# A mixture-of-experts stage on one core: results scattered by tile, later register loads, and three unused matmuls

## What is computed

```python
logits = x @ gate_w + gate_b
probs = jax.nn.softmax(logits, axis=-1)
topv, topi = jax.lax.top_k(probs, K)                 # K = 2 of E = 8 experts
topv = topv / jnp.sum(topv, axis=-1, keepdims=True)
comb = jnp.sum(topv[..., None] * jax.nn.one_hot(topi, E), axis=2)
h = gelu(jnp.einsum('bnd,edf->bnef', x, w1) + b1)    # 192 -> 768
y = jnp.einsum('bnef,efd->bned', h, w2) + b2         # 768 -> 192
ffn_out = jnp.einsum('bne,bned->bnd', comb, y)
out = layernorm(x + ffn_out + bk_scale * (feats @ out_w + out_b))
```

## Time and profile before

| | us |
|---|---|
| median of 3 runs | 229.34 |
| lowest and highest | 228.66 and 230.13 |
| profiled execution, device time | 229.1 |
| its span, first to last instruction | 227.2 |
| PE busy / DVE / POOL / ACT in it | 161.9 / 102.2 / 75.2 / 47.6 |
| mean granted TensorE clock | 0.852 of full |

### The profile page before, as it was taken

How to read it: one execution, slowest core, us unless ns; L and a number is a source line. 1 busy time by engine, 2 the same in 40 slices (tenths; PEclk the granted TensorE clock), 3 DMA queues, 4 the chain that set the end, 5 groups by cost and what they waited for, 6 DMA issues and landing times.

```text
span 227.2 us, 2861 instructions
## 1 busy us (share of the span) xinstructions
PE 161.9 (71%) x928; PEld 133.6 (59%) x928; DVE 102.2 (45%) x302; ACT 47.6 (21%) x89; POOL 75.2 (33%) x196
## 2 busy tenths in 40 slices
PE   0999998888888827610212999999999999993000
PEld 0677754455555415610102899999999999992000
DVE  1129994998899494472103122222332222203445
ACT  0353344343111203210000111232111231110000
POOL 1799300000000121027668877882000000004761
PEclk9999999999999965555555699999999999997555
DMA  6990499999990000003265001000000000011222
GB/s 217 331 408 13 116 265 261 250 261 257 272 341 22 0 1 0 0 0 117 82 197 186 0 5 33 18 19 20 17 31 24 17 20 17 17 38 44 77 56 80
DMA packets 14932, 23.46 MB, mean 103 GB/s; under 512 B 1599, under 2 KB 11396, under 8 KB 14790
## 3 DMA queue, kind: packets, MB, share of 16 engines
q1 hardware_dynamic: 12800, 19.80, 29.9%
q0 software_dynamic: 928, 2.09, 3.0%
q10 hardware_dynamic: 1190, 1.38, 1.9%
HBM read 17.96 MB, written 5.31 MB: 102 GB/s over the span
## 4 chain that ended last, share of the span: by engine, by line
PE 65%; DVE 11%; issue 9%; POOL 5%; DVEq 4%; DMA 3%; ACT 1%; POOLq 0%
PE ps L965 20%; PE ps L975 14%; PE ps L814 8%; PE ps L822 7%; PE ps L823 5%; PE ps L868 4%; POOL diag_s L398 4%; DVEq L746 4%; PE ps L802 3%; DMA w1t_s<-in_w1t 2%; DVE conv L570 1%; DVE stats L616 1%; DVE conv L582 1%; POOL rstd L378 1%; DVE zt L647 1%
## 5 line engine op out<-in xcount | busy, mean ns | idle before, releaser
L965 PE MATMUL ps<-conv 128*128 128x128 f32 x384 | 48.2, 285 | 6.9 <-DVE conv L751 6.5
L965 PEld LDWEIGHTS ps<-conv 128*128 128x128 f32 x384 | 47.3, 201 | 7.6 <-issue 6.8
L570 DVE SCALAR_TENSOR_TENSOR conv<-conv,vecs 128x240 f32<-128x240 f32 (+1 forms) x94 | 35.9, 444 | 7.3 <-ACT conv L447 6.8
L975 PE MATMUL ps<-w_s,conv 128*128 x192 | 33.7, 326 | 0.0
L760 DVE COPY arena<-ps 128x192 f32<-128x192 f32 x16 | 5.7, 358 | 57.5 <-PE ps L975 57.5
L975 PEld LDWEIGHTS ps<-w_s,conv 128*128 128x128 f32 x192 | 30.9, 190 | 0.0
L398 POOL DMA_INDIRECT diag_s<-slot_results,slots x10 | 9.6, 961 | 54.9 <-DMA slot_results<-arena 52.1
L378 POOL TENSOR_TENSOR rstd<-var,neghalf 128x2 f32<-128x2 f32 (+1 forms) x6 | 4.8, 807 | 62.9 <-DVE var L622 62.9
L507 ACT COPY conv<-ps 128x256 f32<-128x256 f32 x16 | 6.0, 373 | 82.8 <-PE ps L956 82.8
L751 DVE COPY conv<-w_s 128x1536 f32 x16 | 15.2, 957 | 14.5 <-issue 9.5
L822 PE MATMUL ps<-conv,pw_s 128*128 128x288 f32 (+1 forms) x48 | 17.4, 445 | 5.5 <-DVE conv L582 3.8
(11 more groups left out here) (152 smaller groups left out, 185.8 us busy)
## 6 DMA issues: line engine op xcount, KB each, us to landing
w_s<-in_w SPq DMA_DIRECT2D x8, 576.0 KB, 18.1
w_s<-in_w SPq DMA_DIRECT2D x8, 384.0 KB
slot_rows<-zero SPq DMA_DIRECT2D x1, 2048.0 KB, 22.2
arena<-in_x SPq DMA_DIRECT2D x4, 432.0 KB, 9.6
w_s<-in_w SPq DMA_DIRECT2D x8, 192.0 KB
slot_results<-arena SPq DMA_DIRECT2D x16, 96.0 KB, 1.6
pw_s<-in_pw SPq DMA_DIRECT2D x1, 1152.0 KB, 11.5
arena<-slot_rows SPq DMA_DIRECT2D x1, 1024.0 KB, 7.6
```

What stands on the lines that cost most here:

```text
L570: ins = nc.vector.scalar_tensor_tensor(out=o, in0=a, scalar=w, in1=o, op0=ALU.mult, op1=ALU.add)
L965: last = mm(p1_ps[i % 2][:, c * P:(c + 1) * P], w1_cur[:, i % 2, k * F + c * P:k * F + (c + 1) * P], xs[:, i % 2, k * P:(k + 1) * P], star ...
L975: last = mm(y_ps[i % 2], hT[:, i % 2, k * P:(k + 1) * P], w2_flat[:, bass.ds(expert[i] * (FK * D) + k * D, D)], start=(k == 0), stop=(k == ...
```

## The change

There are four parts.

1. The destination goes with the row. `ht` becomes one half of `sent`, ScalarE makes the second half, and column 193 carries the row of `yd` where the pair's result belongs: 1 + 2 x token for the first choice, 2 + 2 x token for the second. Slots that hold no pair have a zero there and get a spare row behind all others. When all five pieces of `xg` are there, DVE turns the column into `home`, one destination for each slot.
2. The results are scattered tile by tile. POOL stores the results of tile i with an indirect DMA as soon as they are ready, where SP stored them in slot order. `yd` then lies in token order, and the ten gathers of POOL become plain loads of 192 KB on SP (tiles 0, 2, 4) and ScalarE (tiles 1, 3, and one broadcast row for the class tokens). POOL begins the scatters after its spectral part.
3. The register loads move. PE's 16 come behind the transposes of `combp`; DVE's go into the loop, one ahead of each weight copy.
4. PE multiplies `id_s` by three 384-column slices of `w2_s` into a bank of `p1_ps[1]`, which nobody reads, before it waits for the rows of tile 0.

```diff
--- before.py
+++ after.py
@@ -57,7 +57,8 @@
 
 
 R_TRI, R_ONE, R_THR, R_IOTA, R_VALID = 0, 2 * P, 3 * P, 3 * P + E * E * NT, 3 * P + E * E * NT + S * (E - 1)
-NROUTE = R_VALID + NT * E
+R_HOME, R_SPARE = R_VALID + NT * E, R_VALID + NT * E + 2 * NT
+NROUTE = R_SPARE + S
 
 
 def tower(nc, x, vec, rows, had, w1t, plw, pw, projw, cls, ident, layout, route, w1, b1, w2, b2, outw, xd, yd, out):
@@ -98,7 +99,8 @@
         diag = diag_s[:].rearrange("p (f t m k) -> p f t m k", f=3, t=2, m=3)
 
         zt = sb("zt", [P, NT, D])
-        ht = sb("ht", [P, NT, XW])
+        sent = sb("sent", [P, 2, NT, XW])
+        ht = sent[:, 0]
         stats = sb("stats", [P, NT, 6])
         mv = sb("mv", [P, NT, 2])
         var = sb("var", [P, NT])
@@ -247,6 +253,12 @@
             hi = min(P * (groups[g][-1] + 1), end)
             return slice(lo, hi), slice(0, hi - lo)
 
+        def load_y(queue, t):
+            w = min(P, K1 - t * P)
+            row = 1 + 2 * t * P
+            queue.dma_start(yg[0:w, t, :, :],
+                            yd[row:row + 2 * w, :].rearrange("(p c) d -> p c d", c=2)).then_inc(d_yg[t], 16)
+
         block = ctx.enter_context(nc.Block())
 
 
@@ -274,9 +286,9 @@
             sp.wait_ge(d_sent, 16 * 2 * NT)
             for k, (a, b) in enumerate(pieces):
                 sp.dma_start(xg[:, a:b, :], xd[a * P:b * P, :].rearrange("(i p) c -> p i c", p=P)).then_inc(d_xg[k], 16)
-            for i in range(S):
-                sp.wait_ge(y_rdy, i + 1)
-                sp.dma_start(yd[i * P:(i + 1) * P, :], xg[:, i, 0:D]).then_inc(d_yd, 16)
+            sp.wait_ge(d_yd, 16 * S)
+            for t in (0, 2, NT - 1):
+                load_y(nc.sync, t)
             for t in (0, 2, NT - 1):
                 sp.wait_ge(fin_rdy, t + 1)
                 w = min(P, TOK - P * t)
@@ -361,7 +373,7 @@
                         nc.gpsimd.tensor_scalar(diag[:, f, t, m, :], id_s[:], vecs[:, tap:tap + 1], None,
                                                 ALU.mult).then_inc(diag_rdy, 1)
 
-            nc.gpsimd.memset(ht[:, :, D:XW], 0.0).then_inc(padded, 1)
+            nc.gpsimd.memset(sent[:, :, :, D:XW], 0.0).then_inc(padded, 1)
             nc.gpsimd.memset(combp[:], 0.0).then_inc(padded, 1)
             pool.wait_ge(diag_rdy, 18)
             pool.wait_ge(padded, 2)
@@ -369,8 +381,11 @@
             nc.gpsimd.memset(w1_s[HI, :, 1, :], 0.0).then_inc(w1_zero, 1)
             pool.wait_ge(padded, 3)
             pool.wait_ge(w1_zero, 1)
-            nc.gpsimd.memset(ht[:, :, D:D + 1], 1.0).then_inc(padded, 1)
+            nc.gpsimd.memset(sent[:, :, :, D:D + 1], 1.0).then_inc(padded, 1)
             nc.gpsimd.memset(combp[:, :, SPEC - 1:SPEC], 1.0).then_inc(padded, 1)
+            pool.wait_ge(d_route, 16)
+            nc.gpsimd.tensor_copy(sent[:, :, :, D + 1],
+                                  route_s[:, R_HOME:R_HOME + 2 * NT].rearrange("p (c t) -> p c t", c=2)).then_inc(padded, 1)
 
             def inverse_root(k, grp):
                 ts = (slice(0, 2), slice(2, NT))[grp]
@@ -380,24 +395,25 @@
             for k, grp in enumerate((0, 0, 1, 1)):
                 inverse_root(k, grp)
             pool.wait_ge(d_clear, 16)
-            pool.wait_ge(padded, 5)
+            pool.wait_ge(padded, 6)
             pool.wait_ge(ht_rdy, NT)
+            pool.wait_ge(copied, 1)
             pool.wait_ge(slots_rdy, 2)
             for t in range(NT):
                 w = min(P, K1 - t * P)
                 for c in range(2):
                     nc.gpsimd.indirect_dma_start(
                         out=xd, out_offset=bass.IndirectOffsetOnAxis(ap=slots[0:w, c, t:t + 1], axis=0),
-                        in_=ht[0:w, t, :], in_offset=None).then_inc(d_sent, 16)
+                        in_=sent[0:w, c, t, :], in_offset=None).then_inc(d_sent, 16)
             pool.wait_ge(d_sent, 16 * 2 * NT)
             spectral(pool)
+            pool.wait_ge(home_rdy, 1)
+            for i in range(S):
+                pool.wait_ge(y_rdy, i + 1)
+                nc.gpsimd.indirect_dma_start(
+                    out=yd, out_offset=bass.IndirectOffsetOnAxis(ap=home[:, i:i + 1], axis=0),
+                    in_=xg[:, i, 0:D], in_offset=None).then_inc(d_yd, 16)
             pool.wait_ge(d_yd, 16 * S)
-            for t in range(NT):
-                w = min(P, TOK - t * P)
-                for c in range(2):
-                    nc.gpsimd.indirect_dma_start(
-                        out=yg[0:w, t, c, :], out_offset=None, in_=yd,
-                        in_offset=bass.IndirectOffsetOnAxis(ap=slots[0:w, c, t:t + 1], axis=0)).then_inc(d_yg[t], 16)
             inverse_root(4, 0)
             inverse_root(5, 1)
 
@@ -494,6 +510,9 @@
                 act.wait_ge(xt_mm, 2 * g + 2)
                 nc.scalar.copy(xf[LO, 1, c], xb_ps[g][LO, cp]).then_inc(xf_rdy, 1)
 
+            act.wait_ge(ht_rdy, NT)
+            nc.scalar.copy(sent[:, 1, :, 0:D], ht[:, :, 0:D]).then_inc(copied, 1)
+
             act.wait_ge(lg_max, 1)
             nc.scalar.activation(comb[:], lg[:], ACT.Exp).then_inc(lg_exp, 1)
             act.wait_ge(zeroed, 1)
@@ -512,6 +531,13 @@
                     nc.scalar.activation(hT[:, (i - 1) % 2, :], p1_ps[(i - 1) % 2],
                                          ACT.Gelu_apprx_tanh).then_inc(hT_rdy, 1)
 
+            act.wait_ge(d_yd, 16 * S)
+            row = 1 + 2 * (K1 - 1)
+            act.dma_start(yg[LAST + 1:LAST + B, NT - 1, :, :].rearrange("p c d -> p (c d)"),
+                          yd[row:row + 2, :].rearrange("(o c) d -> o (c d)", o=1).to_broadcast([B - 1, 2 * D])
+                          ).then_inc(d_yg[NT - 1], 16)
+            for t in (1, 3):
+                load_y(nc.scalar, t)
             for t in (1, 3):
                 act.wait_ge(fin_rdy, t + 1)
                 act.dma_start(out[t * P:(t + 1) * P, :], zt[:, t, :]).then_inc(d_out, 16)
@@ -743,16 +769,21 @@
 
             dve.wait_ge(d_w1, 16 * (2 * E + 1))
             dve.wait_ge(tile_e_rdy, 1)
-            expert = [nc.vector.value_load(tile_e[0:1, i:i + 1], min_val=0, max_val=E - 1) for i in range(S)]
 
             def stage_w1(i):
+                expert = nc.vector.value_load(tile_e[0:1, i:i + 1], min_val=0, max_val=E - 1)
                 if i >= 2:
                     dve.wait_ge(p1_mm, i - 1)
                 nc.vector.tensor_copy(w1_cur[:, i % 2, :],
-                                      w1_flat[:, bass.ds(expert[i] * (2 * F), 2 * F)]).then_inc(w1_cur_rdy, 1)
+                                      w1_flat[:, bass.ds(expert * (2 * F), 2 * F)]).then_inc(w1_cur_rdy, 1)
 
             stage_w1(0)
             stage_w1(1)
+            for k in range(len(pieces)):
+                dve.wait_ge(d_xg[k], 16)
+            link(nc.vector.scalar_tensor_tensor(out=home_f[:], in0=xg[:, :, D + 1], scalar=0.0,
+                                                in1=route_s[:, R_SPARE:R_SPARE + S], op0=ALU.is_equal, op1=ALU.mult))
+            nc.vector.tensor_tensor(home[:], home_f[:], xg[:, :, D + 1], ALU.add).then_inc(home_rdy, 1)
             for i in range(S):
                 if i + 2 < S:
                     stage_w1(i + 2)
@@ -765,7 +796,7 @@
 
             def combine(tiles):
                 for t, r in tiles:
-                    dve.wait_ge(d_yg[t], 32)
+                    dve.wait_ge(d_yg[t], 16 if t < q else 32)
                     for c in range(2):
                         dve.wait_ge(v_done, n)
                         own(nc.vector.scalar_tensor_tensor(out=zt[r, t, :], in0=yg[r, t, c, :],
@@ -936,15 +967,17 @@
                           skip_group_check=True)
             last.then_inc(rank_mm, 1)
 
-            pe.wait_ge(tile_e_rdy, 1)
-            expert = [nc.tensor.value_load(tile_e[0:1, i:i + 1], min_val=0, max_val=E - 1) for i in range(S)]
-
             pe.wait_ge(comb_rdy, 1)
             for t in range(NT):
                 last = nc.tensor.transpose(combt_ps[:, t * P:(t + 1) * P], combp[:, t, :], id_s[:])
             last.then_inc(combt_mm, 1)
+            pe.wait_ge(tile_e_rdy, 1)
+            expert = [nc.tensor.value_load(tile_e[0:1, i:i + 1], min_val=0, max_val=E - 1) for i in range(S)]
             pe.wait_ge(d_w2, 16 * E)
             pe.wait_ge(combt_rdy, 1)
+
+            for k in range(3):
+                mm(p1_ps[1][:, 0:F // 2], id_s[:], w2_s[:, k, 0:2, :], start=True, stop=True)
 
             def turn_rows(i):
                 for k, (a, b) in enumerate(pieces):
@@ -1078,7 +1111,10 @@
     route[:, R_THR:R_IOTA] = np.where(e < a, P * k, 1 << 20).reshape(1, -1)
     route[:, R_IOTA:R_VALID] = np.repeat(np.arange(S), E - 1)
     valid = np.arange(NT * P).reshape(NT, P).T < K1
-    route[:, R_VALID:] = np.repeat(valid, E, 1)
+    route[:, R_VALID:R_HOME] = np.repeat(valid, E, 1)
+    token = np.arange(NT * P).reshape(NT, P).T
+    route[:, R_HOME:R_SPARE] = np.concatenate([1 + 2 * token, 2 + 2 * token], 1)
+    route[:, R_SPARE:] = 1 + 2 * K1 + np.arange(S * P).reshape(S, P).T
     arrays = {
```

(8 more changed lines are left out.)

## The result

The median is 217.18 us (215.94 to 218.62, 4 runs) against 229.22 (228.66 to 230.13). The ratio is 0.947, with a 95% interval of 0.941 to 0.954. The kernel was measured twice more beside the experiments, both times at 0.945 (0.943 to 0.947): 216.62 against 229.30, and 216.22 against 228.84. The profiled execution is the fastest of the first four, 215.94 with a span of 214.1, so its rows show a little more gain than the median.

What follows compares the result with a forecast made beforehand. Bound: a chain of waits, with late register loads before the 16 expert tiles and POOL's gathers behind. 229.1 - 4.7 (earlier first product) - 1.9 (clock) - 5.7 (tail) = 216.8, with 0.24 for the median 217.0 us; range 214.6 to 220.6.

Steps and rivals of the forecast that it cites:

- The likeliest case: Whole kernel: earlier first product, clock rising during it and shorter tail give 217.0 us; chance 0.45.
- What bounded the head: Before the first product: register loads on PE and DVE make it late; with both moved, the rows are late next.
- The first product at 118.9: Start of tile 0's first product on PE: about 118.9 instead of 123.59, 4.7 us gained (4.1 to 5.1).
- the collision of the weight copies with the row scatters: Before the first product: DVE's first two weight copies fall inside POOL's row scatters and delay the rows by 1.3 us.
- The delay of 1.9 us: Row scatters on POOL: by the skill's rule each waits for the copy it meets, delay nearer 1.9, sum 0.6 higher.
- The upper bound of 5.1: Gain before the first product if copies cost scatters nothing: rows at 116.5, matmuls cost 0.8 us, at most 5.1 gained.
- The three matmuls: PE before tile 0's rows: 4.1 us, hidden by the wait; clock rises during the first product, 1.9 us gained (0 to 2.6).
- the rival with a chance of 0.17: First product on PE: full clock before it starts, 2.6 us gained in place of 1.9, 216.3 us in all; chance 0.17.
- the first rival: First product on PE: 1.5 us of near idleness undoes the warming, it runs at 1.2 GHz throughout, 218.9 us; chance 0.25.
- DVE's new wait: DVE ahead of the loop: waiting for all row pieces leaves tile 2's weights at 127.2; cost nothing, at worst 1 us.
- The tail: After the last result: scatters and plain loads replace gathers, DVE becomes the bound, 5.7 us gained (4.0 to 6.4).
- POOL's backlog: Result scatters on POOL: over 3.1 us each, POOL sets the end; at 4 us each, 232; chance 0.03.

Runs made afterwards that it cites:

- the kernel with the head alone: Kernel before the change, plus only the later register loads and the three unused matmuls; results still stored by slot and gathered: 222.20 us, ratio 0.969.
- both versions: Changed kernel (without matmuls 217.66 us), and it with DVE's register loads in front, later destinations, ScalarE's tile loads before the broadcast row (214.61; without matmuls 217.24).

## Why the prediction was right

It gave 217.0, and 217.18 came out (216.6 and 216.2 later). The likeliest case was right in its mechanism, and its terms erred in both directions.

*What bounded the head.* Right: the register loads did, and with them gone the rows did. The sum credited both moves, and that was more than the profile supported. Its own rows had the answer: DVE's 16 loads after the early copy at 104 would have ended at 115, before the rows. Either move alone gives the whole gain (A 16.97 and 17.08).

*The first product at 118.9.* It came at 118.29, with the start of the scatters 0.4 later; the gain in A is 5.7 where I said 4.7, outside of my 4.1 to 5.1. The mis-sized term is the collision of the weight copies with the row scatters: 1.3 us predicted, 0.44 to 0.5 measured, and 0.86 in the kernel with the head alone, where one scatter met both copies. The nearest row, small instructions on POOL, was too dear a measure for a scatter of 0.96. The Trainium skill's rule ("SBUF — State Buffer", "SBUF: two separate sides"), that a DMA from GpSimd can't get its descriptors written while such a copy runs, fits: the loss went when the copies did, and in the head-only kernel the scatter of 1.82 us ended at 106.37, just behind the two copies (104.43 to 106.26). The runs show the collision; they don't show that the descriptors are the reason. The delay of 1.9 us that the prediction read out of the rule didn't come: that scatter, 0.96 by itself, ended with the copies and so lost 0.86. The rest of the 1.0 is the transposes of the rows, at full clock: 0.90 us from the rows' transpose to the product in place of 1.07. The upper bound of 5.1 failed because it let the matmuls end at 117.3 and the transposes take 1.07; they ended at 116.75, the clock having risen inside them.

*The three matmuls.* The forecast had the level rise during the first product, worth 1.9 in it; it rose before, and the product gained 2.5. That was the rival with a chance of 0.17. The prediction said that no run shows the point of the rise to vary; now they do, with first products of 4.37 to 5.46 us without the matmuls. The head-only kernel showed the other side: up at 116, half at 120, in part as in the first rival. They cost 3.86 us of PE's time, 4.1 predicted, and lay in the wait for the rows as said.

*DVE's new wait.* Priced at nothing, at worst 1 us; it cost 0.5 to 1.0 in the three traces of the changed kernel. This is the step where the forecast failed in kind: it compared 127.2 with "about 127.2" and took the tie as free. Just the case of full clock, in which PE asks earliest, makes it a cost. The destinations were predicted at 125.2 and came at 125.27, by luck: the collision delayed the rows by 0.5 and not 1.3, but the start was 0.4 later and the last piece took 8.0 us to land, not 7.6.

*The tail.* 5.7 predicted, 5.6 measured, and D is 12.5 to 12.7 us in the three measurements. The first load took 2.6 as taken from the row loads, the last scatter landed 2.31 after its start (2.6 predicted, with an instruction of 1.15 us that took 0.96), and DVE was the bound but for 0.2 to 0.4 of waiting. POOL's backlog was gone with the ninth scatter, long before the end.

*The sum.* Too much for the collision, too little for the clock and nothing for DVE's wait came out at 12.3; the medians moved by 12.0, 12.7 and 12.6. That the first median lies within 0.2 us of the forecast is in part luck: between the two profiled executions the span fell by 13.1. The slower rival, POOL's backlog at over 3.1 us a scatter, was far off at 1.1.

## What to carry to other kernels

When register loads or any other serial block stand between two engines that wait for each other, ask which of the two moves is needed: here one was enough, and moving DVE's as well put copies beside scatters and a load behind a wait. A small instruction with a wait for the last piece of a long transfer belongs behind the work that needs only the first pieces. And measure what a warm-up is worth where nothing else waits at the end of the stretch that it speeds up. The same three matmuls shortened the first product by 2.1 to 2.4 us in both versions, but C by 1.4 to 1.9 in one and by 2.1 in the other; the medians moved by 1.0 and 2.6.

## What was not expected of the hardware

- The granted clock can rise on three unused matmuls and fall again under the real work: full at 116 to 118, half from 120, full again at 123 in the head-only kernel, though the first product had been running without a pause since 118.39. What PE did before the fall was 1.3 us of standing still and then two transposes. The other traces with the matmuls have pauses of 0.3 to 0.8 us or none there, and in them the clock didn't fall. Whether the pause decides is not shown; no kernel varied it alone.
- A row scatter (0.96 us on POOL) beside a DVE copy of 128 x 1536 took 1.11 to 1.82 us; two copies together cost the ten scatters 0.48 or 0.86.
- Without the matmuls, the 24 instructions of the first product took 4.37 to 5.46 us in four traces, so the point at which the clock rises isn't fixed.
- The last piece of the rows, 1024 KB, landed 7.6 to 9.3 us after its issue among the traces, and PE's gap ahead of tile 2 follows it where the destinations stand ahead of that tile's weights: 0.26 us at 8.0, 1.01 us at 8.9, none at 7.8.
- The time to the first row scatter, with nothing changed in it that matters, varied from 99.8 to 101.5 us among the profiled executions.
